# Six images instead of eight beside the sort, 24 more row gathers ahead, and the scan's decay factors in PSUM

## The reference

```python
# block 1, per image, on x normalised over the channels; P = 2304 pixels
xn  = xf / nrm
s   = relu(einsum('bcp,bcq->bpq', xn, xn)) ** 2      # 2304 x 2304 per image
g   = einsum('oc,bcp->bop', Wc, xf) + bc
x   = x + einsum('bpq,bcq->bcp', s, g)
# block 2, on tokens t (M = 32 * 2304 = 73728 rows of 64), normalised
h     = x_flat @ W_gat                                # 16 numbers per token
src, dst = edge_index (262144 edges) + one loop per token
e     = leaky_relu(a_src[src] + a_dst[dst], 0.2)      # 4 heads
ee    = exp(e - segment_max(e, dst)[dst])
agg   = segment_sum(h[src] * ee / denom[dst], dst) + b_gat
w     = softmax(top2(mean over heads(layernorm(agg))))
out   = sum over 4 experts of gate * (gelu(t @ W1 + b1) @ W2 + b2)
```

## Time and profile before

| | us |
|---|---|
| median of three timed runs | 5309.23 |
| profiled execution, its own time | 5277.24 |
| its span, first to last instruction | 5275.0 |
| first block (sort and 8 images), to the barrier | 0 to 1072 |
| merge and routing, first 168 gathers | 1072 to 1410 |
| 24 images | 1410 to 3450 |
| POOL still gathering, the others idle | 3452 to 3563 |
| segment stage with gathers, steps 0 to 19 | 3563 to 4021 |
| segment stage without gathers, steps 20 to 31 | 4021 to 4254 |
| fix-up, gates and experts | 4254 to 5275 |

### The profile page before, as it was taken

One profiled execution on the slowest core, in us unless ns is written; L12 is line 12 of the kernel. 1 busy time (PEld: TensorE's weight loads), 2 busy tenths in 40 slices (PEclk: granted clock), 3 DMA queues, 4 the chain that ended last, 5 costly groups with the idle time before them and its releaser, 6 DMA issues.

```text
span 5275.0 us, 70367 instructions
## 1 busy us (share of the span) xinstructions
PE 3485.0 (66%) x22687; PEld 1462.8 (28%) x22687; DVE 3971.9 (75%) x5512; ACT 3404.4 (65%) x4010; POOL 2951.8 (56%) x2937
## 2 busy tenths in 40 slices
PE   4888988500499999999999999900000017777777
PEld 1223333200244444444444444400000002222222
DVE  8998988997677777777776656606778948778777
ACT  4777988400677777778777787704445626666666
POOL 6000000048777777777777777777774147666661
PEclk9999999755699999999999999955555558898899
DMA  6100100002122222222222222224445526999997
GB/s 259 36 20 20 31 23 16 17 14 83 22 48 58 54 55 55 55 56 50 55 59 52 58 49 53 48 46 143 158 150 194 169 72 137 152 157 158 159 157 151
DMA packets 332471, 441.87 MB, mean 84 GB/s; under 512 B 183193, under 2 KB 261916, under 8 KB 331500
## 3 DMA queue, kind: packets, MB, share of 16 engines
q1 hardware_dynamic: 209744, 288.12, 19.1%
q0 software_dynamic: 105536, 148.61, 16.7%
q10 hardware_dynamic: 16896, 1.18, 0.3%
HBM read 252.35 MB, written 166.47 MB: 79 GB/s over the span
## 4 chain that ended last, share of the span: by engine, by line
POOL 39%; issue 14%; DMA 13%; DVE 8%; PE 3%; ACT 2%; SPq 1%; ACTq 0%; POOLq 0%; DVEq 0%
POOL rows L980 35%; DMA rows<-htab_d,idx 7%; DMA gs<-gates_d 5%; POOL R L1759 2%; PE ye L1931 1%; PE up L1943 1%; DVE S L2508 1%; DVE AD L2493 1%; DVE AE L2487 1%; DVE ms L2630 1%; POOL nb L1716 1%; DMA gates_d<-GH 1%; POOL got L1714 1%; ACT hid L2155 1%; ACT L2155 0%
## 5 line engine op out<-in xcount | busy, mean ns | idle before, releaser
L980 POOL DMA_INDIRECT rows<-htab_d,idx x2048 | 2125.1, 1038 | 668.0 <-issue 594.1
L2063 ACT ACTIVATE rel<-gram 128x1024 f32<-128x1024 f32 (+1 forms) x1080 | 1003.0, 933 | 337.3 <-PE gram L1875 331.5
L2408 DVE SCALAR_TENSOR_TENSOR s<-gram,rel 128x1024 f32<-128x1024 f32 (+1 forms) x720 | 792.6, 1116 | 557.9 <-ACT rel L2063 541.7
L1829 PE MATMUL acc<-s,gT 128*64 128x512 f32 (+1 forms) x4320 | 1028.3, 553 | 0.5 <-issue 0.4
L1875 PE MATMUL gram<-hl 128*64 128x512 f16 (+1 forms) x4320 | 794.3, 365 | 102.4 <-DVE s L2408 59.9
L1875 PE MATMUL gram<-hl,lh 128*64 128x512 f16 (+1 forms) x4320 | 784.6, 361 | 0.0
L1759 POOL DMA_INDIRECT R<-seg_d,nidx x576 | 577.7, 1003 | 195.1 <-issue 169.6
L1080 POOL IOTA slots<- 64x2048 int32 x1 | 1.8, 1833 | 975.5 <-POOLq L192 975.5
L1931 PE MATMUL ye<-hid,w 128*64 128x384 f32 x1536 | 365.9, 555 | 267.9 <-DVE ms L2630 188.9
L1914 PE MATMUL tailsT<-ident,tails 128*20 128x128 f32 x24 | 5.3, 415 | 793.6 <-DVE tails L2516 793.6
L2155 ACT ACTIVATE hid<-up,b1t 128x768 f32<-128x768 f32 x384 | 335.6, 899 | 277.4 <-PE up L1943 266.7
(11 more groups left out here) (372 smaller groups left out, 5429.4 us busy)
## 6 DMA issues: line engine op xcount, KB each, us to landing
gs<-gates_d SPq DMA_DIRECT2D x64, 1024.0 KB, 16.7
rows<-htab_d,idx POOLq DMA_INDIRECT x2048
seg_d<-state SPq DMA_DIRECT2D x32, 996.0 KB, 4.4
raw_d<-w_zeros POOLq DMA_DIRECT2D x48, 512.0 KB, 23.3
raw_d<-rows POOLq DMA_DIRECT2D x32, 768.0 KB, 3.6
tne<-tn_d SPq DMA_DIRECT2D x32, 576.0 KB
x2e<-x_d SPq DMA_DIRECT2D x32, 576.0 KB
out<-res SPq DMA_DIRECT2D x64, 256.0 KB
```

Source lines behind the costliest of these rows:

```text
L980: pool.indirect_dma_start(out=n.rows[:, k % 2, j, :], out_offset=None, in_=n.htabx, in_offset=bass.IndirectOffsetOnAxis(ap=n.idx[:, g % 2, ...
L1829: last = pe.matmul(acc[(par + c) % 2][j * C:(j + 1) * C, 0:w], gT[:, par, 2 * k + j, :], s2[:, u % SLOTS, j * w:(j + 1) * w], start=k == 0 ...
L2063: act.activation(rel[:, t % RELS, 0:2 * w].rearrange("p (j x) -> p j x", j=2), gram[(par + t) % 2][:, :, 0:w], ACT.Relu, scale=1.0 / SPLIT ...
L2408: dve.scalar_tensor_tensor(halves(s2[:, t % SLOTS, 0:2 * w]), gram[(par + t) % 2][:, :, 0:w], 1.0 / SPLIT ** 2, halves(rel[:, t % RELS, 0: ...
```

## The change

Three things are changed. `FIRST` goes from 8 to 6, so six images run in the first block and 26 in the second. The gathers that POOL does before it waits for `img_done` go from 1792 to 1792 + 24 = 1816 (`OVER`). And `G0` is allocated in PSUM (over four of the eight banks, freed before the banks are used for the transposes at the end of the stage) instead of SBUF; since `up0`, which PE's transpose of `b1r` used, lies in the same place, the memset of `G0` comes after a wait for the copy out of it.

```diff
-FIRST = 8
+FIRST = 6
...
     AHEAD = 28
+    OVER = 24
...
-        G0 = ph("G0", [P, NH, NX + 1, CW + 1])
...
+            with ExitStack() as decays:
+                G0 = decays.enter_context(nc.psum_tensor("G0", [P, NH, NX + 1, CW + 1], F32))
...
-            t = AHEAD * GC
+            t = AHEAD * GC + OVER
             gather_rows(pool, n, OPENING, t)
             pool.wait_ge(img_done, 1)
...
             dve.memset(MF[:, :, CW:CW + 1], NEG)
+            dve.wait_ge(v_set, 1)
             dve.memset(G0[:, :, :, 0:1], 0.0)
```

## The result

The changed kernel takes 5651.88 us (median of five, 5646.1 to 5658.2), the kernel before 5309.88 in the runs beside it: ratio 1.0639, 95% interval 1.0618 to 1.0660. That is +342 us; the forecast was 5659 us, +350, in a range of 5605 to 5720. The profiled execution has a span of 5650.1 us.

What follows compares the result with a forecast made beforehand. POOL's gather stream was taken as the bound. First `got` +409, steps with gathers -96 and steps without +37 sum to +350 us; on the timed 5309.2 that gives 5659 us, range 5605 to 5720 with the held-port rival.

Steps and rivals of the forecast that it cites:

- What bounds the kernel: Between 1126 and 4021 us POOL's gather stream sets the time, not the images; moving its start or rate moves the end.
- First part: Six images: first gather waits for image 7, 455 us later; first block 38 us shorter (25 to 55); first `got` +409 with 24 gathers.
- Second part: 24 more gathers before the first `got`: 30 us, within the +409 to the first `got`.
- Third part: `G0` in PSUM, steps with gathers: POOL no longer held at the scan, two steps fewer, 362 instead of 458 us, -96.
- The steps without gathers: After POOL's last gathers: 14 steps at DVE's pace instead of 12, 269 us instead of 232, +37.
- The port stays held: Rival, steps 0 to 17: POOL still held at the scan, or scan slower in PSUM; 416 us, total 5713; 8%.
- my case: The main forecast: steps with gathers take 362 us, total 5659 us, own range 5610 to 5705; 83%.
- The first block set by its images: Rival, first block: PE's images, not DVE's sort, set its length; it ends up to 208 us earlier still, total 5451; 4%.
- The wait does not bind: Rival, first gather: first chunks need six images or fewer, stream starts at 1088, images become the bound, about 5266 us; 3%.
- A faster stream beside the images: Rival, second block: it absorbs the late stream, as by gathers at 1.25 us beside images; 120 us less, 5540; 2%.

Runs made afterwards that it cites:

- six-image run without the wait: Changed kernel with edge source numbers cut to 13 bits, so chunks need images 0 to 3 only (also "the cut sources"): 5234.0 us, 0.9909 of the kernel before.

## Why the prediction was right

**What bounds the kernel.** Right, and shown: the six-image run without the wait takes 5234.0 us where the changed kernel, by its ratio, would take 5279.8 x 1.0639 = 5617 beside it, which was not run there: 383 us, with one pass of the sort's decode between the two programs. The wait on `o_hx` for image 7 is the cause. That no chunk can do with fewer than eight images was read from the reference's `randint` bound, not from any view; the trace of before cannot show it, since the wait was free there.

**First part, with the 24 gathers +409, measured +390.** The first gather came 3 to 6 us behind the second L1584 write of the second block (L1586 in the changed kernel), as said: 4.5 us (1561.9 and 1566.4). The term that was mis-sized is what the first block gives back: 38 us forecast, 53 measured, within the ends I kept. The busy time fell by 35 (916.7 to 881.5), near the 37 worked out. The 16 us more are waits: DVE's on PE and ACT fell from 57 to 40 us. Those for the images fell by 10 where I had 3, and those for the sort's own transposes by 6 where I had a rise of 2:
```profile
DVE edges L316 <- ACT edges L935: 36.0, 18, 5.3
DVE w_half L377 <- PE w_acc L749: 3.8, 2, 2.7
```
Before, the same two rows read 42.0 and 10.4. Why the transposes are waited for less was not looked into. Everything behind it followed: 1351 gathers between 1566 and 3360 us are 1.328 each (1.329 forecast), and after the images 311 were left in 393 us (312 and 393 forecast). The images ended 19 us earlier than forecast, 15 of it the block's.

**Second part.** 24 gathers at 30 us: 32 in the run that has them alone.

**Third part, -96, measured -72.** The steps with gathers took 385.6 us and not 362, 21.4 a step and not 20.1. POOL's groups in them, to be laid beside the earlier trace rows:
```profile
L980 POOL DMA_INDIRECT rows<-htab_d,idx x232 | 236.7, 1020 | 89.6 <-issue 64.9 <-DMA rows<-htab_d,idx 24.7
L1718 POOL DMA_INDIRECT nb<-htab_d,node x18 | 23.2, 1290 | 5.5 <-issue 5.5
L1716 POOL DMA_INDIRECT got<-raw_d,edge x19 | 19.8, 1044 | 5.8 <-issue 5.8
L959 POOL DMA_DIRECT2D raw_d<-rows x4 | 2.4, 588 | 3.9 <-DMA rows<-htab_d,idx 3.9
```
Of the 76 us that POOL's instructions had lost, 25 are still there (1.4 a step, I had left 0.7), and the waits for landings, which the code's limit of four gathers in flight makes, rose from 12.5 to 28.6 where I had 14.

The first of these, some 12 of the 24 us, is a step of the prediction that was wrong: it put both long instructions of the earlier trace rows down to the scan, 3.0 to 3.6 us a step. DVE's row in front of that scan was not shown:
```profile
3606.34 1.53 DVE L2505 TENSOR_TENSOR G<-GT,G 128x1312 f32<-128x1312 f32 x1 [0.54 <-ACT G L2113]
```
This is the product that makes `G1`, with both inputs in SBUF, before and after. The gather of 2.19 us began at 3606.50, inside it; only the `got` of 3.28 us began inside the scan. Over the whole of steps 0 to 19 the time above 0.94 us per instruction is 45 us for the 19 that began in a scan (3.28 or 3.29 us each), 17 for the 19 that began in the product (1.58 to 2.19 each) and 15 for all others. In the changed kernel's steps it is 0 for the 51 that began in 17 scans (0.94 to 0.96 each), 14 for the 17 that began in the product (1.58 to 2.19) and 12 for the others. So PSUM took away the scan's part, all of it, and nothing of the product's, which the prediction had counted with the scan. POOL and DVE in one step:
```profile
3997.24 0.95 POOL L1718 DMA_INDIRECT nb<-htab_d,node  x1 [0.30 <-issue]
3998.49 1.59 POOL L980 DMA_INDIRECT rows<-htab_d,idx  x1 [0.30 <-issue]
4000.39 0.95 POOL L980 DMA_INDIRECT rows<-htab_d,idx  x1 [0.30 <-issue]
4001.64 0.94 POOL L980 DMA_INDIRECT rows<-htab_d,idx  x1 [0.30 <-issue]
...
3997.73 1.53 DVE L2508 TENSOR_TENSOR G<-GT,G 128x1312 f32<-128x1312 f32 x1 [0.54 <-ACT G L2115]
3999.29 3.62 DVE L2511 TENSOR_TENSOR_SCAN S<-G 128x1660 f32<-128x1660 f32 x1
```
The one long row, 1.59 us, begins in the product, which stops at 3999.26; the two rows behind it begin in the scan, from 3999.29 to 4002.91, and take 0.95 and 0.94. Both rows go with the rule that was cited from the Trainium skill ("SBUF — State Buffer", "SBUF: two separate sides"): two SBUF inputs hold GpSimd. The section adds a condition that the prediction left out, that with two SBUF inputs this holds only against a GpSimd instruction that reads SBUF; these gathers have their row numbers (`idx`) there, and no run here has one that reads none.

The waits for landings go with the decays in PSUM too: over the steps with gathers they are 22.6 us in the run with that part alone, against 12.5 before and 13.5 with six images alone. That a POOL which is held less often reaches its limit of four sooner is the likely reason; no run changed the limit.

The steps without gathers took 268.5 us (269 forecast), and the scan and the exponential lost nothing by `G0` in PSUM: 3.62 as before, and 1.52 instead of 1.55 us:
```profile
4436.22 1.52 ACT L2116 ACTIVATE G<-X 128x1640 f32<-128x1640 f32 x1
```

**The rivals.** The port stays held: out for the scan, by the rows above and by the run with PSUM alone; but POOL is still held at the product, and the steps' 386 us lie between the 362 of my case and the 416 of this rival. The first block set by its images: out, it gave back 53 us and not 246. The wait does not bind: out for this input; with the cut sources it is what happens, and the time worked out for it, 43 us under before, was measured as 46. A faster stream beside the images: out, 1.328.

**What cancelled.** Up to the last scan, the first `got` came 19 us earlier than forecast (15 of it from the first block), and the steps took 24 us longer; that the sum came within 4 us (354 against 350) is luck in part, as each term was only right to within 25 us. Behind the last scan I had put nothing and the trace has 21 us, which the baseline of 5309, 32 us above the profiled execution, made good: luck again.

What stays open: why the waits for landings are there at all at about one place per step, behind the fetches of `got` and `nb`; and why the last part took 1042 us in the changed kernel's trace. More gathers in flight were not tried.

## What to carry to other kernels

Before work is moved from one stage to a later one, ask what else waits for its result: here the later stage had room for two more images (without the wait the first `got` came at 3553, and at 3563 before), but the rows of one of them open the gather stream. With six images alone the stream opened 440 us later, and 352 of them were lost. A wait that is free in the trace does not show there; its condition has to be worked out from the code and the data. And where a serial engine feeds a stage, doing more ahead is not a gain by itself: starting the stage as soon as its inputs allow (1704 gathers ahead) won 75 us together with the decays in PSUM, which alone won 38, where 24 more ahead lost 26. Last, when a slow instruction overlaps two instructions of another engine, look at which of them was running as it began. Here each long instruction belonged to the one that it began in, and only the scan's came back.

## What the runs showed of the hardware

- An indirect DMA's instruction on POOL, 0.94 us when nothing holds it, takes 3.28 us when it begins in a scan of two SBUF tensors (19 of 19 in the kernel before), and 0.94 to 0.96 in the same scan with one of them in PSUM (51 of 51 after); the scan takes 3.62 us either way.
- One that begins in a product of two SBUF tensors (1.53 us) takes 1.6 to 2.2 us, in both kernels.
- An exponential of 1640 elements takes 1.52 us into PSUM and 1.55 into SBUF.
- A gather's pace is 1.26 us with nothing beside it, 1.33 beside the images and 1.69 in the merge. Beside the images it is the same for rows from 8192 and from 16384 table entries.
- The last part of the program, in which DVE waits most for the landing of `gs`, took 1016 to 1042 us in the traces, with the same instructions.
